# A scatter stage in which VectorE takes two steps over from GpSimd, in a new order, and a program block that ends without GpSimd's drain

## The chip, the cores and the metric

The kernel runs on one core of one Trainium2 chip. The metric is the device time in microseconds (us) of one execution. The engines are TensorE (PE in the profile; its weight loads are PEld), VectorE (DVE), ScalarE (ACT), GpSimd (POOL) and SyncE (SP, which here issues DMA transfers). Each engine runs its own instruction list in order, and the lists meet only through semaphores. A name with a q behind it (POOLq, SPq) is the engine's sequencer.

## The reference, cut to what matters

The input is x of shape (32, 128, 128): 32 batches of 128 tokens with 128 features. A graph-attention block of four rounds conditions x, then comes one transformer layer with a mixture of experts, and x is added to its result:

```python
ctx = cond(x, ...)                                   # four rounds of graph attention
a   = layernorm(ctx + mha(ctx), ln1_g, ln1_b)        # 16 heads
gp  = softmax(a @ w_group + b_group)                 # 4 groups, best one taken
ep  = softmax(einsum('td,gde->tge', a, w_expert) + b_expert)   # 2 experts in each
combine = one_hot(g_idx * 2 + e_idx) * (g_prob * e_prob)
h   = relu(einsum('td,edf->etf', a, w1) + b1)
y   = einsum('etf,efd->etd', h, w2) + b2
out = x + layernorm(a + einsum('te,etd->td', combine, y), ln2_g, ln2_b)
```

Each token uses one expert of eight. The kernel therefore sorts the tokens by expert and computes only the chosen expert for each.

## The kernel before, in words

Tokens are handled in batches of 128 (B = 32) and groups of four batches (GB = 4, G = 8). Groups are numbered 0 to 7 in the code, so G - 3 is group 5 (the sixth), G - 2 is group 6 and G - 1 is group 7. The stages are:

- The four rounds of graph attention.
- The attention of the transformer layer, a software pipeline over the batches (`for u in FLOW`). For a batch v, PE makes scores and weighs values, ACT takes exponentials (`exponentials`), DVE divides by the sums (`normalise`, L1722 and L1724), PE turns the heads (`turn_heads`, L1229, in front of it `turn_outputs`, L1224) and multiplies by the output weights with the residual (`residual`, L1238 and L1243). DVE copies that out (`residual_out`, L1733) and takes its statistics (`norm1_stats`, L1739).
- For each group of four batches: the variance (`norm1_variance`, L1744, DVE), the power -1/2 of it (`norm1_power`, L719 and L723, POOL), the normalised rows xn (`norm1_out`, L2288, ACT), and a chain of 20 small DVE steps called `route` that picks each token's expert and computes its row number `slot_i`. The links 12 and 13 (L1823, L1828) give the row number, the links 14 to 16 (L1832, L1834, L1837) the token's weight, the links 17 to 19 the running counts.
- A token's row is written to `rows`: xn times ln1_g (the x1g step), plus ln1_b (the x1 step), beside x plus bias (which `load_rows` on SP brought from DRAM) and the token's number (`group_ids`, L743). For groups 0 to 5 POOL makes x1g and x1 (L731, L734, function `rows_x1` of the gpsimd part), for groups 6 and 7 DVE (L1852, L1859, functions `rows_x1g` and `rows_x1` of the vector part). Then POOL scatters the four batches of the group into `sorted_rows` in DRAM, one indirect DMA for each (`scatter`, L761).
- The table: when five groups are counted, DVE computes where the first 13 tiles (FIRST) of 128 sorted rows lie (`tile_ends`, `tile_rows`, L1898 to L1903); POOL derives some ends from it (`taken_ends`, L832 to L845). When all are counted, DVE computes the other 26.
- The experts: 39 tiles. SP loads a tile (`load_tile`, L541), PE and ACT run the two layers, DVE adds and normalises (L2047 to L2073), and POOL scatters the tile's rows to the output with one indirect DMA (L870), 39 in all. At the very end SP waits until all of them have landed (L557), and the block ends with a barrier of all engines (its instructions carry line L117 in the profile).

All orders are written out by hand in the source. POOL's and DVE's lists behind the FLOW loop are what the change touches. SP's list at this point is: `load_rows(5)`, `load_rows(6)`, a wait for the first table, seven `load_tile`, `load_rows(7)` (it waits until group 5 is scattered), six `load_tile`, a wait for the second table and for all scatters, and the other 26.

Of the kernel before, what the change touches and what calls it, by code (L numbers as in the profile page):

```python
# [14 lines left out]
B, N, D = 32, 128, 128  # L15
TOK = B * N
GB = 4
G = B // GB
# [47 lines left out]
FIRST = -((EXPERTS * (N - 1) - COUNTED * GT) // N)  # L66
# [46 lines left out]
def build(nc, x, xT, adj, mask, weights, rowvecs, consts, ids, w1, w2, b2, out):  # L113
# [3 lines left out]
    with ExitStack() as ctx:  # L117
# [159 lines left out]
        t_base = sb("t_base", [128, FIRST])  # L277
# [117 lines left out]
        def S(name):  # L395

            if name not in sems:
                sems[name] = sem(name)
            return sems[name]
# [87 lines left out]
            copy(qkx[:, bs, :, TYPES:QK], vb[:, :, D + TYPES:D + TYPES * (1 + T_ITER)]  # L487
                 .rearrange("p b (t i) -> p b t i", i=TYPES)).then_inc(read, 1)

        block = ctx.enter_context(nc.Block())  # L490

        @block.sync
        def _(sp):
# [66 lines left out]
        def _(pool):  # L560
# [153 lines left out]
            def norm1_power(p):  # L714

                pool.wait_ge(S("mv_ready"), p + 1)
                if p >= 1:
                    pool.wait_ge(S("rstd_ready"), p)
                pool.tensor_scalar(ve[:, :], mv[:, :, 1], EPS, None, ALU.add).then_inc(S("var_ready"), 1)  # L719
                pool.wait_ge(S("var_ready"), p + 1)  # L720
                if p >= 1:
                    pool.wait_ge(S("xn_ready"), p)
                pool.tensor_tensor(rstd[:, :], ve[:, :], C("half"), ALU.pow).then_inc(S("rstd_ready"), 1)  # L723

            def rows_x1(p):

                if p == G - 3:
                    pool.wait_ge(S("on_ready"), B - 3)
                pool.wait_ge(S("xn_ready"), p + 1)
                bc = lambda n: R(n).unsqueeze(1).broadcast_to([128, GB, D])  # L730
                pool.tensor_tensor(x1_g[:, :, :], xn[:, :, :], bc("ln1g"), ALU.mult).then_inc(S("x1g_ready"), 1)  # L731
                pool.wait_ge(S("x1g_ready"), p + 1)
                pool.wait_ge(S(f"in_rows{p % 2}"), 16 * (p // 2 + 1))
                pool.tensor_tensor(rows[:, p % 2, :, 0:D], x1_g[:, :, :], bc("ln1b"), ALU.add).then_inc(S("row_x1"), 1)  # L734
# [6 lines left out]
            def group_ids(p):  # L741

                pool.tensor_copy(rows[:, p % 2, :, 2 * D + 1:2 * D + 2].bitcast(I32),  # L743
                                 id_s[:, p * GB:(p + 1) * GB].unsqueeze(2)).then_inc(S("row_ids"), 1)
# [84 lines left out]
            def taken_ends():  # L829

                pool.wait_ge(S("table_chain"), FIRST_ENDS)
                pool.memset(upto_first[:, 0:1], 0.0).then_inc(S("taken_chain"), 1)  # L832
                pool.memset(taken[:, EXPERTS:EXPERTS + 1], 0.0).then_inc(S("taken_chain"), 1)
                pool.tensor_scalar(upto_first[:, 1:EXPERTS + 1], cum[:, :], float(FIRST), None, ALU.min)\
                    .then_inc(S("taken_chain"), 1)
                pool.wait_ge(S("taken_chain"), 3)
                pool.tensor_tensor(taken[:, 0:EXPERTS], upto_first[:, 1:EXPERTS + 1], upto_first[:, 0:EXPERTS],
                                   ALU.subtract).then_inc(S("taken_chain"), 1)
                pool.wait_ge(S("taken_chain"), 4)
                pool.tensor_tensor(turn[:, :], taken[:, 1:EXPERTS + 1], taken[:, 0:EXPERTS], ALU.subtract)\  # L840
                    .then_inc(S("taken_chain"), 1)
                pool.wait_ge(S("taken_chain"), 5)
                pool.tensor_scalar(turn[:, :], turn[:, :], float(N), float(REGION), ALU.mult, ALU.add)\
                    .then_inc(S("taken_chain"), 1)
                pool.tensor_scalar(t_base_later[:, :], C("tile")[:, 0:LATER], taken[:, 0:1], float(N), ALU.add, ALU.mult)\  # L845
                    .then_inc(S("taken_chain"), 1)

            rows_x1(G - 3)
            taken_ends()
            group_ids(G - 3)  # L850
            norm1_power(G - 2)
            for n in range(GB):
                scatter(G - 3, n)
            pool.wait_ge(S("scattered0"), 16 * GB * (G // 2 - 1))
            group_ids(G - 2)
# [629 lines left out]
        def _(dve):  # L1485
# [227 lines left out]
            def normalise(v):  # L1713

                if v >= 1:
                    dve.wait_ge(S("on_ready"), v)
                if v >= 2:
                    dve.wait_ge(S("on_mm"), v - 1)
                dve.wait_ge(S("oq_mm"), v + 1)
                o = (OQ_LAST if v == B - 1 else OQ).rearrange("p (k c) -> p k c", c=STRIP)[:, :, 0:PAIR * VW].rearrange("p k (s c) -> p k s c", s=PAIR)  # L1720
                inverse = rden[:, :].rearrange("p (k s) -> p k s", s=PAIR)
                dve.reciprocal(inverse, o[:, :, :, HD]).then_inc(S("rden_ready"), 1)  # L1722
                dve.wait_ge(S("rden_ready"), v + 1)
                dve.tensor_tensor(o_n[:, v % 2, :].rearrange("p (k s c) -> p k s c", s=PAIR, c=HD), o[:, :, :, 0:HD],  # L1724
                                  inverse.unsqueeze(3).broadcast_to([128, HEADS // PAIR, PAIR, HD]), ALU.mult)\
                    .then_inc(S("on_ready"), 1)

            def residual_out(v):
                g, b = divmod(v, GB)
                if b == 0 and g >= 2:  # L1730
                    dve.wait_ge(S("xn_ready"), g - 1)
                dve.wait_ge(S("h_mm"), v + 1)
                dve.tensor_tensor(h_s[:, g % 2, b, :], head_bank(v), rowv[:, RCOLS["bo"][0]:RCOLS["bog"][1]], ALU.add)\  # L1733
                    .then_inc(S("h_ready"), 1)

            def norm1_stats(v):
                g, b = divmod(v, GB)
                dve.wait_ge(S("h_ready"), v + 1)
                dve.bn_stats(stats[:, b, :], h_s[:, g % 2, b, 0:D]).then_inc(S("stats_ready"), 1)  # L1739
# [149 lines left out]
            def tile_ends(n):  # L1889

                then(dve.tensor_reduce(cum[:, :], ntu[:, :, :], AX_X, ALU.add))
                then(dve.tensor_tensor(behind[:, 0:n, :], C("tile")[:, 0:n].unsqueeze(2).broadcast_to([128, n, EXPERTS]),
                                       row8(cum[:, :], n), ALU.is_ge))
                then(dve.tensor_reduce(t_exp[:, 0:n], behind[:, 0:n, :], AX_X, ALU.add))
# [56 lines left out]
            for u in FLOW:  # L1951
                nxt, b, more = group(u, 1)
                done, _, whole = group(u, -1)
                norm, _, normed = group(u, -2)
                if batch(u + LEAD):
                    row_tops(u + LEAD)
                if u == -1:
                    gate_centred()
                if u == 0:
                    gate_folded()  # L1960
                if batch(u - 4):
                    residual_out(u - 4)
                if b in (1, 2) and more and nxt > 0:
                    value_out(nxt, Y0, b - 1)
                if b == 2 and normed:
                    if norm == COUNTED - 1:
                        first_counts()
                    route(norm, range(12, 13))
                if u == B - GB - 1:
                    first_full(1)  # L1970
                if u == B - GB:
                    dve.wait_ge(S("st_mm"), 2 * (B - GB))
                    tile_sums()
                if batch(u - 2):
                    normalise(u - 2)
                if batch(u - 4):
                    norm1_stats(u - 4)
                if b == 0 and normed:
                    norm1_logits(norm)
                    route(norm, range(0, 6))  # L1980
                if b == 1 and normed:
                    route(norm, range(6, 12))
                if b == 2 and normed:
                    route(norm, range(13, ROUTE))
                if b == 3 and whole:
                    norm1_variance(done)
                if 1 <= u <= 4:
                    bias_parts(u - 1)
                if u == B - GB - 2:
                    first_full(0)  # L1990
                if u == B - GB - 1:
                    first_full(2)
                if u == B - GB + 1:
                    tile_ends(FIRST)
            residual_out(B - 6)
            route(G - 3, range(12, 14))
            norm1_stats(B - 6)
            normalise(B - 4)
            route(G - 3, range(14, 17))
            tile_rows(0, FIRST, t_base)  # L2000
            route(G - 3, range(17, ROUTE))

            residual_out(B - 5)
            norm1_stats(B - 5)
            norm1_variance(G - 2)
            normalise(B - 3)

            normalise(B - 2)
            norm1_logits(G - 2)
# [436 lines left out]
```

## Time and profile before

| what | value |
|---|---|
| median of 3 runs | 520.4 us (519.62 to 520.53) |
| the profiled execution's own time | 520.18 us |
| its span in the profile | 518.4 us |
| PE busy | 480.2 us (93%) |
| DVE busy | 419.3 us (81%) |
| ACT busy | 384.1 us (74%) |
| POOL busy | 274.1 us (53%) |

The span is the time from the first to the last instruction that the profile holds; 1.78 us of the execution's own time lie outside it. The busy shares are means over stages with different limits: PE is at its limit in the first 400 us, and in the last 60 us all engines are busy in turns. The page also says that the granted TensorE clock was 9 tenths or more in all slices but the last.

### The profile page before, as it was taken

To read this page: it belongs to the slowest core of one execution; us is meant where nothing else is said; L and a number is where in the kernel's file an instruction comes from. 1 tells how busy PE (TensorE), PEld (TensorE's weight loads), DVE (VectorE), ACT (ScalarE), POOL (GpSimd) and SP (SyncE) were. 2 spreads that over 40 slices of the span, in tenths; PEclk is the share of its full clock that TensorE was granted. 3 is DMA by queue.
4 is the path that set the end of the run, shared out by engine and by line. 5 is a ranking of instruction groups with operands and counts; after the bars stand their busy time and mean duration, and the time that the engine had idled before them with its cause. 6 is when DMAs were issued, how large, how long until landed. Compare 5 with 4: busy or idle time off the path is not lost. (4 is left out here: it accounts for less than half of the span.)

```text
span 518.4 us, 14957 instructions
## 1 busy us (share of the span) xinstructions
PE 480.2 (93%) x4946; PEld 327.3 (63%) x4946; DVE 419.3 (81%) x1163; ACT 384.1 (74%) x1157; POOL 274.1 (53%) x468
## 2 busy tenths in 40 slices
PE   5999999999999999999999999999999988889990
PEld 3765666766676777666545456565565655779880
DVE  2589898888888888899866768787887888899892
ACT  3779778888887888877846767677776757779990
POOL 0486673333322233302814446588887876777774
PEclk9999999999999999999999999999999999999996
DMA  8800899999999300050240000001012411555530
GB/s 344 353 2 3 258 296 301 301 292 292 295 302 295 104 0 0 2 162 1 118 126 2 3 1 3 3 33 43 24 53 54 185 44 52 151 157 146 151 106 10
DMA packets 49955, 65.64 MB, mean 127 GB/s; under 512 B 2509, under 2 KB 45522, under 8 KB 48736
## 3 DMA queue, kind: packets, MB, share of 16 engines
q1 hardware_dynamic: 47104, 58.42, 38.7%
q0 software_dynamic: 2784, 6.37, 3.5%
q8 instruction: 37, 0.61, 0.5%
q14 instruction: 30, 0.25, 0.2%
HBM read 21.04 MB, written 44.19 MB: 126 GB/s over the span
## 5 line engine op out<-in xcount | busy, mean ns | idle before, releaser
L1709 DVE TENSOR_REDUCE nm<-SC 128x8 f32<-128x1024 f32 x64 | 75.4, 1220 | 26.3 <-PE SC L1174 25.6
L2256 ACT ACTIVATE room_p<-ST 128x512 f32<-128x512 f32 (+1 forms) x96 | 64.0, 739 | 35.0 <-PE ST L1193 35.0
L1607 DVE TENSOR_REDUCE room_w<-SC 128x512 f32<-128x2048 f32 x32 | 73.0, 2281 | 1.2 <-PE SC L1001 1.2
L625 POOL TENSOR_TENSOR spread<-parts,units 128x48 bf16<-128x48 bf16 x32 | 8.8, 277 | 121.3 <-DVE parts L1582 121.3
L2162 ACT ACTIVATE room_w<-room_w,shift 128x128 f32<-128x128 f32 x128 | 49.7, 390 | 16.6 <-DVE shift L1616 16.5
L2153 ACT ACTIVATE room_w<-ST,cv 128x128 f32<-128x128 f32 x128 | 36.4, 365 | 17.7 <-PE ST L1016 17.7
L870 POOL DMA_INDIRECT out<-room_v x39 | 38.3, 982 | 12.2 <-issue 8.5
L1016 PEld LDWEIGHTS ST<-room_w 128*128 128x128 f32 x256 | 33.0, 191 | 14.2 <-issue 13.0
L761 POOL DMA_INDIRECT sorted_rows<-room_w,slot_i x32 | 33.3, 1040 | 16.2 <-issue 12.7
L2171 ACT ACTIVATE room_w<-room_w,inv 128x128 f32<-128x128 f32 x128 | 41.0, 407 | 0.1
L969 PE MATMUL ST<-room_w 128*128 128x136 f32 x256 | 40.3, 280 | 0.2 <-POOL room_w L609 0.2
L1187 PE MATMUL ST<-room_v,room_w 32*128 32x512 f32 x256 | 36.5, 638 | 2.9 <-DVE room_w L1698 1.6
L671 POOL TENSOR_TENSOR ctx_t<-room_w 128x512 f32<-128x512 f32 x24 | 30.5, 1271 | 12.0 <-PE SC L1001 8.5
L769 POOL TENSOR_TENSOR room_v<-room_w,cst 128x512 f32<-128x512 f32 x28 | 28.9, 1043 | 13.5 <-PE SC L1174 11.6
L1174 PE MATMUL SC<-room_v,room_w 32*128 32x512 f32 x256 | 35.5, 617 | 0.0
L969 PEld LDWEIGHTS ST<-room_w 128*128 128x128 f32 x256 | 34.4, 190 | 1.5 <-issue 1.5
L1016 PE MATMUL ST<-room_w 128*128 128x128 f32 x256 | 34.2, 277 | 0.9 <-issue 0.9
L1214 PE MATMUL SC<-room_p,room_w 128*32 128x128 f32 x992 | 33.5, 276 | 0.4 <-ACT room_p L2256 0.4
L1052 PE MATMUL ST<-room_w,w 128*128 128x512 f32 x64 | 33.0, 597 | 0.7 <-ACT room_w L2153 0.7
L964 PE MATMUL ST<-room_w,ctx_t 128*128 128x136 f32 x192 | 30.1, 279 | 0.0
L1214 PEld LDWEIGHTS SC<-room_p,room_w 128*32 128x32 f32 x992 | 25.2, 109 | 5.2 <-ACT room_p L2256 1.2
L1009 PEld LDWEIGHTS ST<-cst,room_w 128*128 128x128 f32 x128 | 15.5, 141 | 18.0 <-ACT room_w L2171 14.1
(340 smaller groups left out, 1327.0 us busy)
## 6 DMA issues: line engine op xcount, KB each, us to landing
sorted_rows<-w SPq DMA_DIRECT2D x8, 4290.0 KB, 38.3
room_v<-sorted_rows SPq DMA_DIRECT2D x39, 130.0 KB
x_t<-xT SPq DMA_DIRECT2D x2, 1024.0 KB, 8.2
ctx_t<-adj SPq DMA_DIRECT2D x1, 2048.0 KB, 16.8
biased_rows<-room_w SPq DMA_DIRECT2D x2, 1024.0 KB, 4.3
room_w<-biased_rows SPq DMA_DIRECT2D x8, 256.0 KB, 3.4
room_w<-mask SPq DMA_DIRECT2D x1, 1536.0 KB, 19.8
w<-weights SPq DMA_DIRECT2D x1, 1356.0 KB, 8.8
```

Of the source, the lines that this page charges most:

```text
L870: pool.indirect_dma_start(out, bass.IndirectOffsetOnAxis(ap=number, axis=0), fin[:, t % OUTS, :], None, bounds_check=TOK - 1, oob_is_err=F ...
L969: mm = pe.matmul(V[:, b, 0:D + QK], plpc[:, g % 2, b * N:(b + 1) * N], w_v[:, g % 2, b, 1, :], start=opens(s) and b in (0, 3), stop=not op ...
L1016: mm = pe.matmul(M[:, b, :], v_s[:, g % 4, b, :], prob_t[:, b, :], start=True, stop=True)
L1174: mm = pe.matmul(SC[:, r, :], q_s[at, g % 2, b * N:(b + 1) * N], k_m[at, g % 2, :, b * N:(b + 1) * N], start=True, stop=True)
L1187: pe.matmul(ST[:, r, :], k_s[at, g % 2, b * N:(b + 1) * N], q_m[at, g % 2, :, b * N:(b + 1) * N], start=True, stop=False)
L1214: mm = pe.matmul(to[STRIP * j:STRIP * (j + 1), half * N:(half + 1) * N], v_a[:, g % 2, b, at:at + STRIP], ex[:, v % 2, r, i * N:(i + 1) * ...
L1607: dve.tensor_reduce(logit[:, :, :], SC[:, :, :].rearrange("p b (i m) -> p b m i", i=TYPES), AX_X, ALU.max)\
L1709: dve.tensor_reduce(nm[:, v % 2, 2 * PER_R * pair:2 * PER_R * (pair + 1)], SC[:, 2 * pair:2 * pair + 2, :].rearrange("p r (i n) -> p (r i) ...
L2153: op = act.activation(msg_s[:, b * N:(b + 1) * N], M[:, b, :], ACT.Copy, scale=scale)
L2162: op = act.activation(expo[:, b, :], leaky[:, b, :], ACT.Exp, bias=shift[:, b:b + 1], accum_out=total[:, b:b + 1])
L2171: op = act.activation(prob[:, b, :], expo[:, b, :], ACT.Copy, scale=inv[:, b:b + 1])
L2256: act.activation(ex[:, v % 2, first:last, :], ST[:, first:last, :], ACT.Exp)\
```

## The change

The edits are:

- `Block(no_gpsimd_drain=True)`: the end of the block, a barrier of all engines, no longer has a drain on GpSimd; the other engines keep theirs.
- POOL no longer makes the x1g and x1 steps of group 5, nor waits there for `on_ready`. DVE makes them: x1g ahead of `residual_out(B - 6)`, x1 behind `norm1_stats(B - 6)` and ahead of `normalise(B - 4)`.
- On DVE `tile_rows(0, FIRST, t_base)` moves from ahead of `residual_out(B - 5)` to behind `norm1_variance(G - 2)`, and the links 17 to 19 of `route(G - 3)` move to behind `normalise(B - 3)`.
- On POOL the first scatter of group 5 moves ahead of `norm1_power(G - 2)`. `group_ids(G - 3)` gets a wait of its own until group 3 is scattered.

```diff
-        block = ctx.enter_context(nc.Block())
+        block = ctx.enter_context(nc.Block(no_gpsimd_drain=True))
...
             def rows_x1(p):
-                if p == G - 3:
-                    pool.wait_ge(S("on_ready"), B - 3)
                 pool.wait_ge(S("xn_ready"), p + 1)
...
-            rows_x1(G - 3)
             taken_ends()
+            pool.wait_ge(S("scattered1"), 16 * GB * (G // 2 - 2))
             group_ids(G - 3)
+            scatter(G - 3, 0)
             norm1_power(G - 2)
-            for n in range(GB):
+            for n in range(1, GB):
                 scatter(G - 3, n)
...
+            rows_x1g(G - 3)
             residual_out(B - 6)
             route(G - 3, range(12, 14))
             norm1_stats(B - 6)
+            rows_x1(G - 3)
             normalise(B - 4)
             route(G - 3, range(14, 17))
-            tile_rows(0, FIRST, t_base)
-            route(G - 3, range(17, ROUTE))

             residual_out(B - 5)
             norm1_stats(B - 5)
             norm1_variance(G - 2)
+            tile_rows(0, FIRST, t_base)
             normalise(B - 3)
+            route(G - 3, range(17, ROUTE))
```

## Rows read from the trace of the kernel before

**Rows 1.** Instructions at the block's end, line 117: ns min/median/max, first and last start us.

```profile
L117 POOLq DRAIN  x1: 8715/8715/8715, 509.4 to 509.4; - x1
...
L117 SPq DRAIN  x1: 13/13/13, 513.8 to 513.8; - x1
...
L117 SPq EVENT_SEMAPHORE  x1: 17/17/17, 518.3 to 518.3; - x1
```

**Rows 2.** POOL's timeline from 457 us: start us, us, instruction, idle before and releaser.

```profile
457.00 0.99 POOL L761 DMA_INDIRECT sorted_rows<-room_w,slot_i  x1 [1.12 <-DVE room_w L1837]
...
511.30 0.97 POOL L870 DMA_INDIRECT out<-room_v  x1 [0.30 <-issue]
```

**Rows 3.** DVE's timeline, its last instruction.

```profile
508.52 0.35 DVE L2068 SCALAR_TENSOR_TENSOR room_v<-room_v,rs 128x128 f32<-128x128 f32 x1
```

**Rows 4.** DVE's timeline from 435 to 443 us.

```profile
435.13 0.30 DVE L1733 TENSOR_TENSOR room_w<-SC,rowv 128x140 f32<-128x140 f32 x1 [0.79 <-PE SC L1243]
...
435.87 0.24 DVE L1722 RECIPROCAL rden<-SC 128x16 f32<-128x16 f32 x1
...
436.54 1.26 DVE L1834 SCALAR_TENSOR_TENSOR den<-ee,gs 128x4 f32<-128x4 f32 x1
...
437.93 1.33 DVE L1898 TENSOR_TENSOR room_v<-room_v,hop 128x104 f32<-128x104 f32 x1
...
439.89 0.17 DVE L1903 TENSOR_SCALAR exp_i<-t_exp 128x13 int32<-128x13 f32 x1
...
440.48 0.29 DVE L1733 TENSOR_TENSOR room_w<-SC,rowv 128x140 f32<-128x140 f32 x1
...
441.13 0.38 DVE L1744 BATCH_NORM_AGGREGATE mv<-stats 128x2 f32<-128x6 f32 x4
...
442.67 0.26 DVE L1722 RECIPROCAL rden<-SC 128x16 f32<-128x16 f32 x1 [0.69 <-PE SC L1229]
```

**Rows 5.** POOL's timeline from 434 to 444 us.

```profile
434.29 0.97 POOL L761 DMA_INDIRECT sorted_rows<-room_w,slot_i  x1 [0.30 <-issue]
436.52 1.26 POOL L731 TENSOR_TENSOR room_w<-room_w,rowv 128x512 f32<-128x512 f32 x1 [1.26 <-DVE room_w L1724]
437.86 1.28 POOL L734 TENSOR_TENSOR room_w<-room_w,rowv 128x512 f32<-128x512 f32 x1
...
440.53 0.29 POOL L845 TENSOR_SCALAR t_base_later<-cst,taken 128x26 f32<-128x26 f32 x1
...
441.92 1.05 POOL L723 TENSOR_TENSOR rstd<-ve,cst 128x4 f32<-128x4 f32 x1
443.16 1.13 POOL L761 DMA_INDIRECT sorted_rows<-room_w,slot_i  x1 [0.20 <-issue]
```

**Rows 6.** PE's timeline from 437 to 443 us.

```profile
437.50 0.40 PE L1243 MATMUL SC<-w,room_w 128*128 128x140 f32 x2
...
440.83 0.33 PE L1229 MATMUL SC<-cst,room_w 128*128 128x128 f32 x1 [1.54 <-DVE room_w L1733]
...
442.10 0.44 PE L1224 MATMUL SC<-cst,room_w 128*128 128x128 f32 x2
```

**Rows 7.** ACT's timeline, the xn rows of group 5.

```profile
429.73 1.65 ACT L2288 ACTIVATE room_w<-room_w,shift,rstd 128x128 f32<-128x128 f32 x4
```

**Rows 8.** DVE's timeline, the same operations at other places.

```profile
448.03 0.16 DVE L1834 SCALAR_TENSOR_TENSOR den<-ee,gs 128x4 f32<-128x4 f32 x1
...
452.75 0.69 DVE L1852 TENSOR_TENSOR room_w<-room_w,rowv 128x512 f32<-128x512 f32 x1
453.77 0.69 DVE L1859 TENSOR_TENSOR room_w<-room_w,rowv 128x512 f32<-128x512 f32 x1 [0.32 <-DMA room_w<-biased_rows]
...
461.23 0.34 DVE L1898 TENSOR_TENSOR room_v<-room_v,hop 128x208 f32<-128x208 f32 x1
```

**Rows 9.** POOL's timeline beside the DVE rows at 452.75 us.

```profile
452.12 0.98 POOL L761 DMA_INDIRECT sorted_rows<-room_w,slot_i  x1 [0.30 <-issue]
```

**Rows 10.** SP's timeline, the first seven tile loads.

```profile
441.06 7.71 SPq L541 DMA_DIRECT2D room_v<-sorted_rows  x7
```

## The prediction

> **What bounds the kernel now.** I read the page first, then the end of the timeline, then the waits and the timelines of each engine from 430 to 465 us, where the edits lie.
>
> The end has two parts. The first is the last step of the program. DVE's last result is ready at 508.52 + 0.35 = 508.87 [rows 3]; POOL issues the last output transfer at 511.30 and is done with it at 512.27 [rows 2]. SP, which waits until all outputs have landed, executes its own drain at 513.8. Yet the closing barrier comes at 518.3, because POOL's drain began at 509.44 and took 8.715 us, until 518.16 [rows 1]. So 4.5 us at the end are a wait of four idle engines for one drain, 4.3 of them removable if SP's 513.8 plus a short barrier becomes the end.
>
> The second part is what brings POOL to 512.27. From the scatter at 457.00 to the one at 511.30 there are 42 steps (three more scatters, 39 outputs) in 54.30 us, that is 1.293 us each against 0.97 of execution and 0.30 between two [rows 2]. POOL thus has no slack of its own from 457.00 on: the end is 457.00 plus a fixed train. The start of the train waited 1.12 us for a DVE reciprocal (the last link of group 7's route) [rows 2]. Its forerunner is DVE's list, which hardly idles from 435 on: the waits that stand there are 0.79 at 435.13, 0.69 at 442.67 and 0.32 at 453.77 [rows 4, 8]. So the bound of this stretch is DVE, and what shortens DVE between 434 and 443 should bring the whole tail forward.
>
> Two DVE instructions there are far too long. The 4-element step L1834 takes 1.26 at 436.54 and 0.16 elsewhere [rows 4, 8]. It runs in the same time as POOL's 128x512 product (436.52, 1.26) [rows 5]. The step L1898 takes 1.33 on 104 elements at 437.93, beside POOL's second product (437.86, 1.28), and 0.34 on 208 elements at 461.23 [rows 4, 5, 8]. DVE is held while POOL runs these. The excess is 1.10 and about 1.03 (I take 0.30 for 104 elements): 2.1 us.
>
> **The block's end.** The drain of POOL goes, the others stay. POOL's engine work ends at 512.27, before SP's 513.8, so SP sets the end. Between POOL's drain end (518.16) and SP's event at 518.3 lie 0.15 to 0.2 [rows 1]; the new end is 513.8 + 0.2 = 514.0. Gain 4.3. Bounds: nothing, if what the drain does is paid behind the span instead; 4.4 at most. I take 4.3, since no other instruction in the trace waits for it. The 1.78 us outside the span are taken as unchanged.
>
> **x1g on DVE.** One instruction of 0.69, about 0.71 with its hand-over [rows 8]. Its input xn is ready at 431.38 [rows 7], so it starts where DVE now idles, 434.34, and ends near 435.05. The residual copy behind it waits for PE until 435.13 anyway [rows 4]. Cost nothing; if that cover were gone, 0.7.
>
> **x1 on DVE.** 0.69 again [rows 8], between the statistics and `normalise(B - 4)`, which starts at 435.87 now [rows 4] and moves to about 436.5. It waits for the loaded rows, but link 13 ahead of it already waits for the same load. Cost 0.7. PE needs that result only behind the weighing of batch B - 2, which follows the matmuls that end at 437.90 [rows 6]; the 0.7 are hidden for PE.
>
> **POOL's products gone.** DVE loses the two holds. The route's links 14 to 16 follow: L1837 ends at 437.56, where it now ends at 438.01. DVE then reaches `residual_out(B - 5)` by 437.6. PE closes that bank at 437.50 + 0.40 = 437.90 [rows 6], so the copy starts at 438.0 and not at 440.48 [rows 4]: 2.5 us earlier, of which about 1.7 come from the table being behind it now.
>
> **PE's wait.** `turn_heads(B - 4)` sits behind that copy: PE idles 1.54 and starts at 440.83 [rows 6]. It came free at 440.83 - 1.54 = 439.29, and now finds the copy done at 438.3. The wait vanishes. Then comes `weigh(B - 1)`, about one microsecond of matmuls (it fits between the rows at 440.83 and 442.10), 439.4 to 440.5 if ACT's exponentials for it are ready, then `turn_outputs(B - 2)` at 440.6 and not at 442.10 [rows 6]. It also needs `normalise(B - 3)`.
>
> **DVE's new order.** Copy 438.0, statistics 438.3, variance 438.65 to 439.0 (0.38 [rows 4]), then the table: 0.3 + 0.3 + 0.2 + 0.1 + 0.2, done at 440.0. It ends at 439.89 + 0.17 = 440.06 today [rows 4], so the first tile loads, at 441.06 with 1.1 us each (7.71 for seven [rows 10]), neither gain nor lose. `normalise(B - 3)` follows, done at 440.5, just in time for PE at 440.6, then the links 17 to 19 until 441.0, in the time in which DVE waits for PE. `normalise(B - 2)` starts at 441.15 and not at 442.67 [rows 4]. That is the gain: 1.5 us, and what is behind it on DVE has no idle time until the first tiles.
>
> **POOL.** Its scatter of group 4 ends at 435.26 [rows 5]. `taken_ends` runs 439.14 to 440.82 now, 1.7 us [rows 5], and will run 435.3 to 437.0. The added wait for group 3's scatters is met long before (group 4's are already being issued). Then `scatter(G - 3, 0)` waits for link 16 (437.56): start about 438.4 (0.8 behind it, my value between the idle 0.20 before the scatter at 443.16 and the 1.12 before the one at 457.00 [rows 2, 5]), end 439.5. Behind this wait stand `norm1_power(G - 2)` and the other scatters. The variance is there at 439.0, the power runs 439.9 to 441.0 (1.05), where it ended at 442.97 [rows 5]. DVE wants it at about 441.65. Slack 0.6. The other three scatters end near 444.6, 3.5 us earlier than now, which also sends `load_rows(7)` out earlier and should remove most of the 0.32 for which DVE waits at 453.77 [rows 8]. That gives the end 0 to 0.3 more.
>
> **A rule that speaks against it.** DVE's product at 452.75 took 0.69 with a POOL scatter in progress from 452.12 to 453.10 [rows 8, 9]: no hold. In the Trainium skill, SBUF — State Buffer, section "SBUF: two separate sides", a VectorE copy in a two-port mode locks GpSimd out so that it cannot write descriptors (its figure, an estimate here: about 620 ns become 3,100). By that rule a scatter could be 2.5 us late; the moved steps are products of two SBUF inputs, and this trace shows no such hold, so the sum leaves it out.
>
> **The sum.** Span 518.4 - 4.3 - 1.5 = 512.6. Own time 520.18 - 5.8 = 514.4. The median lies 0.2 above the profiled execution, so 514.6.
>
> **Rivals.**
>
> - *Both as above*: 514.6. For it: each wait named is in the trace. Against it: it needs PE, POOL and DVE to be in step at 440.5 to 441. Its own range is 513.6 (reorder 2.4, the most that the variance's advance gives) to 515.6. Chance 0.62.
> - *The order gives little*: the tail hangs on something else than DVE, for example the first tile loads. Tile 0 is issued at 441.06 as before and each further one 1.1 later [rows 10], while PE would ask for them 1.5 earlier than now; no row shows when one lands, and if the loads are just in time today, this part shrinks to 0.5 or nothing. Time 515.6 to 516.2. Or the power on POOL is late by more than its slack of 0.6. Chance 0.17.
> - *The drain's time is only partly saved*, because the work it did is done outside the span. If it is paid in parallel to what else lies there, nothing of the 4.3 is gained: 520.4 - 1.5 = 518.9. For it: the drain worked 5.9 us beyond POOL's last instruction (518.16 - 512.27), and beyond SP's, so it does something real. Against it: no row says that anybody needs it. Chance 0.11. The Trainium skill, Runtime: NRT & Kernel Launch, section "The ~15µs preamble/postamble breakdown", says that a launch ends with a barrier of all engines and a re-arming of the DMA rings; no row here shows these.
> - *Slower: the same work starts only behind the barrier.* Then it is not even in parallel with the last landing. Place: right behind the span. Price 5.9 if it is the part beyond POOL's last instruction, 8.7 if the whole record. With 5.9 the time is 514.6 + 5.9 = 520.5, the same as before; with 8.7 it is 523.3. It decides from a price of 6.8 on (5.8 gained, and 1.0 to be told from no change). Chance of the same 0.06, of slower 0.04.
>
> **How the numbers follow.** A difference of 0.2% (1.0 us) is about what a measurement of this kernel tells from no change. Faster: 0.62 + 0.17 + 0.11 = 0.90, same 0.06, slower 0.04. The range: from 513.4 (reorder 2.4, and 0.2 of the load wait) to 517.5. It holds the first two cases and a drain of which a third is still paid; left out are the 0.21 of the last two rivals.
>
> **What would show it.** Right: a span of about 512.6, no POOL drain at the block's end, L1834 and L1898 at 0.16 and 0.30, the copy of batch B - 5 at 438.0, the PE wait of 1.54 gone, `normalise(B - 2)` at 441.15, the train of scatters starting at 455.4. Wrong about the end: own time minus span above 1.78 by several us. Wrong about the order: the first L1834 of the tail or DVE's `normalise(B - 2)` stays, or the train starts at 456.5 or later though DVE is early; then the tile loads or POOL's power hold it.

## The result, and the profile after

The changed kernel takes 514.28 us (median of 4 runs, 513.47 to 514.57); the kernel before took 520.07 in the same comparison. The ratio is 0.9886, with a 95% interval from 0.9869 to 0.9903: 1.1% faster. The profiled execution has a span of 512.4 and an own time of 514.35, so 1.95 lie outside the span (1.78 before).

The end of the program first. These are the instructions of line 117 in the changed kernel, as in [rows 1]:

```profile
L117 SPq EVENT_SEMAPHORE  x2: 17/17/17, 512.2 to 512.4; - x2
L117 POOLq EVENT_SEMAPHORE  x2: 17/17/17, 512.2 to 512.3; - x2
...
L117 SPq DRAIN  x1: 13/13/13, 512.1 to 512.1; - x1
```

No row of a POOL drain is left. From SP's drain at 512.1 to the end of the span are 0.3 us, where it was 513.8 to 518.4. Of the 6.0 us by which the span is shorter, 4.3 lie here and 1.7 ahead of it.

Now POOL's timeline in the changed kernel, with group 5's first scatter, the power of group 6, the first scatter of group 6, the start of the train, and the last output:

```profile
438.84 1.08 POOL L759 DMA_INDIRECT sorted_rows<-room_w,slot_i  x1 [0.89 <-POOL room_w L741]
440.00 0.25 POOL L719 TENSOR_SCALAR ve<-mv 128x4 f32<-128x4 f32 x1
440.33 1.05 POOL L723 TENSOR_TENSOR rstd<-ve,cst 128x4 f32<-128x4 f32 x1
...
449.24 1.13 POOL L759 DMA_INDIRECT sorted_rows<-room_w,slot_i  x1 [1.74 <-DVE dg L1797]
...
455.43 0.98 POOL L759 DMA_INDIRECT sorted_rows<-room_w,slot_i  x1 [0.98 <-DVE room_w L1836]
...
509.67 0.97 POOL L869 DMA_INDIRECT out<-room_v  x1 [0.31 <-issue]
```

The train starts at 455.43, 1.57 earlier than in [rows 2], and ends at 510.64, 1.63 earlier: 42 steps in 54.24 us, as before (54.30).

VectorE's timeline in the changed kernel, against [rows 4] and [rows 8]:

```profile
434.70 0.69 DVE L1851 TENSOR_TENSOR room_w<-room_w,rowv 128x512 f32<-128x512 f32 x1
435.39 0.30 DVE L1732 TENSOR_TENSOR room_w<-SC,rowv 128x140 f32<-128x140 f32 x1
...
436.13 0.68 DVE L1858 TENSOR_TENSOR room_w<-room_w,rowv 128x512 f32<-128x512 f32 x1
...
437.40 0.16 DVE L1833 SCALAR_TENSOR_TENSOR den<-ee,gs 128x4 f32<-128x4 f32 x1
...
438.20 0.30 DVE L1732 TENSOR_TENSOR room_w<-SC,rowv 128x140 f32<-128x140 f32 x1 [0.42 <-PE SC L1242]
...
439.16 0.23 DVE L1897 TENSOR_TENSOR room_v<-room_v,hop 128x104 f32<-128x104 f32 x1
...
441.32 0.26 DVE L1721 RECIPROCAL rden<-SC 128x16 f32<-128x16 f32 x1
...
452.20 0.69 DVE L1858 TENSOR_TENSOR room_w<-room_w,rowv 128x512 f32<-128x512 f32 x1 [0.47 <-DMA room_w<-biased_rows]
```

The idle 0.79 ahead of the residual copy is filled by x1g. L1833 (L1834 before) is at 0.16 where it was 1.26, and the table's first product at 0.23 where it was 1.33. The copy of batch B - 5 starts at 438.20. `normalise(B - 2)` starts at 441.32 and not at 442.67. This execution reached the stretch 0.33 us later than the one before (group 4's last scatter starts at 434.62, against 434.29 in [rows 5]), so the stretch gained 1.7. The 0.42 ahead of the copy of batch B - 5 is a new wait, for PE. The last row shows a wait that grew: 0.47 where it was 0.32.

PE in the changed kernel, against [rows 6]:

```profile
439.10 0.44 PE L1223 MATMUL SC<-cst,room_w 128*128 128x128 f32 x2
439.38 0.27 PE L1228 MATMUL SC<-cst,room_w 128*128 128x128 f32 x1
...
440.74 0.44 PE L1223 MATMUL SC<-cst,room_w 128*128 128x128 f32 x2
```

The wait of 1.54 us ahead of `turn_heads(B - 4)` is gone.

SP in the changed kernel: the load of group 6's rows and of group 5's (the first row), seven tile loads, `load_rows(7)`, the other tile loads:

```profile
421.18 16.27 SPq L524 DMA_DIRECT2D room_w<-biased_rows  x2
441.38 7.50 SPq L541 DMA_DIRECT2D room_v<-sorted_rows  x7
448.93 0.43 SPq L524 DMA_DIRECT2D room_w<-biased_rows  x1
```

The tile loads start at 441.38 (441.06 before, [rows 10]); `load_rows(7)` stands right behind the seventh.

### The profile page after: what moved, and what is told of

Same layout as the page of the kernel before. It is cut to its first block and busy times, and to the rows that moved or that the text cites. A ratio compares the mean times of both kernels' runs of the same rounds, so it can differ in the third digit from the quotient of the medians.

```text
span 512.4 us, 14960 instructions
## 1 busy us (share of the span) xinstructions
PE 480.3 (94%) x4946; PEld 327.7 (64%) x4946; DVE 418.4 (82%) x1165; ACT 383.7 (75%) x1157; POOL 271.8 (53%) x466
```

## The experiments

Times are medians; each ratio is against the kernel before on the same chip, and a gain by the ratio can differ by 0.2 us from the difference of the medians. "Rows" below means the x1g and x1 steps of group 5.

### 1. The block's end alone

The kernel before with `nc.Block(no_gpsimd_drain=True)` and nothing else.

```diff
-        block = ctx.enter_context(nc.Block())
+        block = ctx.enter_context(nc.Block(no_gpsimd_drain=True))
```

Expected:

> The kernel before with the one edit at the block's end (no GpSimd drain). Theory (the drain is a wait of its own, and nobody pays it later): span 518.4 - 4.3 = 514.1, time 4.3 us below before, some 515.8, and still 1.8 to 1.9 us between span and own time. Rival (its work moves outside the span): the span falls just as much, but own time minus span grows to 6 us and the time stays at 520. Rival (part of it was hidden by the order edits): less than 3.5 us gained here.

Measured: 515.84 against 520.22, ratio 0.9922 (0.9905 to 0.9938). The span is 513.9, the own time 515.84, so 1.94 lie outside. That is a gain of 4.4 us: all of the 4.3 are gained here, and nothing is paid later. The rival that moves the drain's work outside the span is refuted: 1.94 against 1.78 is 0.2, not 4.

### 2. The order alone, with the drain

The changed kernel with the first line of its diff taken back.

```diff
-        block = ctx.enter_context(nc.Block(no_gpsimd_drain=True))
+        block = ctx.enter_context(nc.Block())
```

Expected:

> The changed kernel with GpSimd's drain put back: all edits of order and the two steps on VectorE, nothing else. Theory (the two parts add up): 1.6 us below before, some 518.5; POOL's drain again ends about 5.9 us behind its last instruction. Rival (the order matters only because the drain is gone, as the drain started earlier hides it): no change. If the first part gave 4.3 and this 1.6, the sum is the 5.8 measured.

Measured: 519.05 (10 runs, 517.73 to 520.12), ratio 0.9977 (0.9966 to 0.9989): 1.2 us, between 0.6 and 1.8. The profile has a span of 516.5, 1.9 shorter. The two parts add up: 4.4 and 1.2 against 5.8 measured for both in the first comparison and 6.1 in the later one. The drain in this kernel:

```profile
L117 POOLq DRAIN  x1: 9318/9318/9318, 506.9 to 506.9; - x1
```

and POOL's last instruction in it:

```profile
509.40 0.97 POOL L869 DMA_INDIRECT out<-room_v  x1 [0.30 <-issue]
```

The drain ends at 516.2, 5.9 behind the end of that instruction (510.37), as before (518.16 - 512.27). Its record begins 3.5 us ahead of that end (before: 2.8), so the length of the record, 9.3 or 8.7, also holds time in which POOL still issued transfers.

### 3. Only the rows on VectorE

The kernel before, with drain, old place of the table, old order of the scatters.

```diff
-                if p == G - 3:
-                    pool.wait_ge(S("on_ready"), B - 3)
...
-            rows_x1(G - 3)
             taken_ends()
+            pool.wait_ge(S("scattered1"), 16 * GB * (G // 2 - 2))
             group_ids(G - 3)
...
+            rows_x1g(G - 3)
             residual_out(B - 6)
             route(G - 3, range(12, 14))
             norm1_stats(B - 6)
+            rows_x1(G - 3)
             normalise(B - 4)
```

Expected:

> The kernel before (drain kept, table and scatters in the old order) with only the rows of the sixth group made by VectorE, x1g ahead of residual_out(B - 6), x1 behind norm1_stats(B - 6). Theory (the holds of VectorE by POOL's products were the cost): L1834 falls to 0.16 and L1898 to 0.3 us, the table is ready at 438.8, normalise(B - 2) starts about 441.5, and 1.1 of the 1.6 us come from this edit alone. Rival (the order of table and variance is what pays): normalise(B - 2) stays near 442.5 and under 0.4 us are gained.

Measured: 518.43, ratio 0.9962 (0.9948 to 0.9975): 1.8 us by the medians, 2.0 by the ratio, more than the 1.1 expected and no less than the whole order gave. VectorE's timeline in it:

```profile
437.05 0.16 DVE L1832 SCALAR_TENSOR_TENSOR den<-ee,gs 128x4 f32<-128x4 f32 x1
...
437.34 0.23 DVE L1896 TENSOR_TENSOR room_v<-room_v,hop 128x104 f32<-128x104 f32 x1
...
438.81 0.29 DVE L1731 TENSOR_TENSOR room_w<-SC,rowv 128x140 f32<-128x140 f32 x1
...
441.00 0.26 DVE L1720 RECIPROCAL rden<-SC 128x16 f32<-128x16 f32 x1 [0.69 <-PE SC L1227]
```

The copy of batch B - 5 comes at 438.81, 0.9 later than where the changed kernel has it (438.20, less its 0.3 of lateness), and yet `normalise(B - 2)` starts at 441.00, as early. VectorE has 0.69 of idle ahead of it: PE is not ready sooner. So the new place of the table fills an idle time that costs nothing.

### 4. What holds VectorE: a first try that does not decide

The kernel before, where L1834 has one input. It leaves the factor gs out of the tokens' weights.

```diff
-                        op = dve.scalar_tensor_tensor(den[:, :], ee[:, :], 1.0, gs[:, :], ALU.add, ALU.mult)
+                        op = dve.tensor_scalar(den[:, :], ee[:, :], 1.0, None, ALU.add)
```

Expected:

> The kernel before, where L1834 (den) has one input in place of two: it leaves the factor gs out, so the tokens' weights are not the reference's. POOL's two 128x512 products stay. Theory (an instruction of VectorE with two SBUF inputs is held while POOL runs its product): L1834 takes 0.16 us, and the hold moves on to the next VectorE instruction with two SBUF inputs, L1898, or falls away where POOL's first product has ended by then; the second product then meets whatever has two inputs. Rival (VectorE is held whatever it runs): L1834 still takes 1.26.

Measured, in VectorE's timeline of this kernel:

```profile
436.68 1.26 DVE L1834 TENSOR_SCALAR den<-ee 128x4 f32<-128x4 f32 x1
437.98 0.18 DVE L1837 RECIPROCAL room_w<-den 128x4 f32<-128x4 f32 x1
438.07 1.32 DVE L1898 TENSOR_TENSOR room_v<-room_v,hop 128x104 f32<-128x104 f32 x1
```

Held as before: the theory as I put it, by the number of inputs alone, has failed. It did not decide between the number of inputs and the kind of the instruction: the one that I had put in is of another kind than the one it replaces. The reciprocal, with one input too, ran its 0.18 free, but it began at 437.98, 0.02 ahead of POOL's second product (438.00 to 439.28), so it shows little by itself.

### 5. The same with a reduction

L1834 becomes a sum over eg; the tokens' weights are again other ones.

```diff
+                        op = dve.tensor_reduce(den[:, :], eg[:, :, :], AX_X, ALU.add)
```

Expected:

> The kernel before, where L1834 (den) is a TENSOR_REDUCE over eg with its one input in SBUF, so the tokens' weights are not the reference's; the previous try used a TENSOR_SCALAR, which was held for 1.26 us too, although it has one input. Theory A (what is held is an instruction that takes VectorE's second path into SBUF: two inputs, or a TENSOR_SCALAR or copy in a faster mode; a reduction is not): L1834 takes 0.17, L1837 0.18 behind it, and L1898, now ahead of POOL's first product's end, is held until that ends (0.5 to 0.9 us). Theory B (VectorE is held whatever it runs): L1834 takes 1.26 again.

Measured. VectorE's timeline:

```profile
436.47 0.17 DVE L1834 TENSOR_REDUCE den<-eg 128x4 f32<-128x16 f32 x1
436.67 0.18 DVE L1837 RECIPROCAL room_w<-den 128x4 f32<-128x4 f32 x1
436.77 1.06 DVE L1898 TENSOR_TENSOR room_v<-room_v,hop 128x104 f32<-128x104 f32 x1
437.87 0.26 DVE L1899 TENSOR_REDUCE t_hop<-room_v 128x13 f32<-128x104 f32 x1
438.16 0.93 DVE L1900 TENSOR_TENSOR t_row<-t_hop,t_base 128x13 f32<-128x13 f32 x1
...
447.62 0.69 DVE L1852 TENSOR_TENSOR room_w<-room_w,rowv 128x512 f32<-128x512 f32 x1
...
449.97 0.16 DVE L1777 SCALAR_TENSOR_TENSOR shift<-mv,rstd 128x4 f32<-128x4 f32 x1 [0.94 <-POOL rstd L723]
```

POOL's timeline in the same kernel:

```profile
436.44 1.26 POOL L731 TENSOR_TENSOR room_w<-room_w,rowv 128x512 f32<-128x512 f32 x1 [1.26 <-DVE room_w L1724]
437.79 1.28 POOL L734 TENSOR_TENSOR room_w<-room_w,rowv 128x512 f32<-128x512 f32 x1
...
447.63 0.76 POOL L719 TENSOR_SCALAR ve<-mv 128x4 f32<-128x4 f32 x1
448.48 1.46 POOL L723 TENSOR_TENSOR rstd<-ve,cst 128x4 f32<-128x4 f32 x1
...
452.85 1.47 POOL L761 DMA_INDIRECT sorted_rows<-room_w,slot_i  x1 [0.30 <-issue]
```

Theory A holds to the number. The reduction and the reciprocal run free beside POOL's first product. The hold moves on to L1898 and ends with that product (437.83 against 437.70), and a new one falls on L1900, which ends at 439.09 with the second product (439.07). The reduction between them, L1899, runs free. So two-input instructions, and in experiment 4 the TENSOR_SCALAR, wait until POOL's product ends; reductions and reciprocals don't.

The time is 520.16, the span 518.4, as before, although VectorE was 0.67 us earlier at `normalise(B - 2)` (442.00 against 442.67). The last VectorE row says where that went: at 449.97 it waits 0.94 for POOL's power of group 7. The rows of the kernel before at this place are

```profile
449.99 0.16 DVE L1777 SCALAR_TENSOR_TENSOR shift<-mv,rstd 128x4 f32<-128x4 f32 x1 [0.22 <-POOL rstd L723]
```

for VectorE and

```profile
448.29 0.27 POOL L719 TENSOR_SCALAR ve<-mv 128x4 f32<-128x4 f32 x1
448.63 1.32 POOL L723 TENSOR_TENSOR rstd<-ve,cst 128x4 f32<-128x4 f32 x1
```

for POOL. POOL came to this power 0.66 us earlier too (447.63 against 448.29), and yet ends it at 449.94, as before (449.95). Now it is POOL that is held: VectorE's product of group 6 began at 447.62, 0.01 ahead of L719, which takes 0.76 in place of 0.27; L723, which begins during VectorE's next product, takes 1.46. In the kernel before L719 began 0.04 ahead of that product (448.33) and was free. Further on, a scatter that begins at 452.85, 0.06 behind another product of VectorE (452.79), takes 1.47 in place of 0.97. So most of what VectorE gained was lost because POOL's steps ran into VectorE's products. This experiment does not show that POOL's list by itself would have held the gain back. It shows how much slack that list has: ahead of the power of group 6 POOL waited 0.65 for VectorE's variance in the kernel before (until 441.61), and here it does not wait (440.95).

### 6. The rows alone, without the drain

The kernel of experiment 3, and

```diff
-        block = ctx.enter_context(nc.Block())
+        block = ctx.enter_context(nc.Block(no_gpsimd_drain=True))
```

Expected:

> The kernel before with the rows of the sixth group on VectorE and without GpSimd's drain, all other order as before. The run with the rows alone gave 1.8 us, the whole order 1.2. Theory (the new order of table and first scatter adds nothing to the rows): the same time as the changed kernel in this call, within 0.5 us, some 514.3. Rival (the new order adds its part): 0.5 to 1 us slower than the changed kernel.

Measured: 514.27 (513.61 to 515.48), ratio 0.9887 (0.9868 to 0.9907).

### 7. The table back in its old place

The changed kernel with

```diff
             route(G - 3, range(14, 17))
+            tile_rows(0, FIRST, t_base)
+            route(G - 3, range(17, ROUTE))
             residual_out(B - 5)
             norm1_stats(B - 5)
             norm1_variance(G - 2)
-            tile_rows(0, FIRST, t_base)
             normalise(B - 3)
-            route(G - 3, range(17, ROUTE))
```

Expected:

> The changed kernel with the first table's rows and the counts back ahead of residual_out(B - 5); the first scatter stays ahead of the power. Theory (the late table holds SP's first seven loads, and so the load of group 7's rows, for which VectorE waited 0.47 us at L1858): the first tile load goes out 1.3 us earlier, load_rows(7) at 447.2 in place of 448.9, VectorE's wait goes, and 0.3 to 0.5 us are gained on the changed kernel. Rival (the earlier variance is worth more): the variance comes 0.6 us later, the power with it, and the time is equal or 0.5 us longer.

Measured: 514.89 (514.51 to 515.32), ratio 0.9894 (0.9876 to 0.9911). VectorE's wait at L1858 is gone, as expected, but no time is gained. POOL's timeline in this kernel:

```profile
452.04 1.36 POOL L759 DMA_INDIRECT sorted_rows<-room_w,slot_i  x1 [0.30 <-issue]
453.71 0.97 POOL L759 DMA_INDIRECT sorted_rows<-room_w,slot_i  x1 [0.30 <-issue]
...
455.77 0.99 POOL L759 DMA_INDIRECT sorted_rows<-room_w,slot_i  x1 [0.88 <-POOL room_w L741]
```

and VectorE's:

```profile
451.86 0.69 DVE L1858 TENSOR_TENSOR room_w<-room_w,rowv 128x512 f32<-128x512 f32 x1
```

The earlier product now begins ahead of a scatter, and the scatter takes 1.36 in place of 0.97. It ends 0.85 behind the product's end (452.55), so it was held for 0.4. The train starts at 455.77, later than in the changed kernel. In experiment 6, with the table in its old place too, the scatter begins at 451.98, 0.05 ahead of the product (452.03), and takes 0.97.

### 8. The changed kernel again

Without any edit. Expected:

> The changed kernel itself, unchanged, for comparison on the same chip as the two above: 5.8 us below before, some 514.3, as in its first measurement.

Measured: 514.09 (513.75 to 515.80), ratio 0.9883 (0.9865 to 0.9902). So experiments 6 and 8 can't be told apart: 514.27 and 514.09, with runs 1.9 and 2.1 us apart. Experiment 7, at 514.89, lies 0.8 above this median, and five of the six runs here are faster than all of its five; the intervals of the ratios overlap, so that it is slower is likely and not shown. The theory of experiment 6 stands: the new place of the table and of the first scatter adds nothing that can be measured to the rows alone.

### 9. Group 7's rows loaded one tile earlier

```diff
-                if k == FIRST // 2:
+                if k == FIRST // 2 - 1:
                     load_rows(7)
```

Expected:

> The changed kernel, with the load of group 7's rows issued by SP behind six tile loads in place of seven. Theory (two engines are level here: VectorE's wait of 0.24 to 0.47 us at L1858 for these rows goes, but POOL's own list, four scatters, group_ids and 0.88 us until the next scatter, starts the train no earlier): VectorE's wait at L1858 gone, the train still starts within 0.2 of 455.1, time equal within 0.3 us. Rival (VectorE alone sets the train): the train starts 0.4 us earlier and the time falls by 0.4.

Measured: 514.79 (513.92 to 515.66), ratio 0.9898 (0.9880 to 0.9915). The wait at L1858 is gone, the train starts at 455.73 (expected within 0.2 of 455.1, so later than that). Again a scatter runs into the product (it takes 1.35 at 452.00, the product runs from 451.82).

### 10. And group_ids(G - 1) ahead

```diff
-            for n in range(GB):
-                scatter(G - 2, n)
+            scatter(G - 2, 0)
             pool.wait_ge(S("scattered1"), 16 * GB * (G // 2 - 1))
             group_ids(G - 1)
+            for n in range(1, GB):
+                scatter(G - 2, n)
             for n in range(GB):
                 scatter(G - 1, n)
```

Expected:

> The run above, and group_ids(G - 1) on POOL moved from behind the four scatters of group 6 to behind the first of them, so that the next scatter can follow after 0.30 us. Theory (both level engines are now relieved): the train starts at 454.5 to 454.7 in place of 455.1 to 455.4, and the time falls by 0.3 to 0.6, which the measurement can just tell. Rival (the 39 tiles of PE, ACT and VectorE are level with the train too; in the changed kernel POOL waits for VectorE's result in 22 of the 39 steps): the train starts earlier and ends as before, time unchanged.

Measured: 514.61 (513.61 to 514.89), ratio 0.9889 (0.9871 to 0.9908). The train starts at 455.39. This profiled execution was 0.47 us later than that of the changed kernel from 434 on (group 4's last scatter at 435.09 against 434.62). With that taken off, the train starts 0.5 earlier than in the changed kernel (454.9 against 455.43) and ends 0.1 earlier (511.03 less 0.47, against 510.64). That looks like the rival's picture, in which the 39 tiles on PE, ACT and VectorE are level with POOL's train and a train that starts earlier waits inside. It is not shown, though: the profile names VectorE's result as the releaser of 20 of the 39 outputs (22 in the changed kernel), but nearly all of them follow after the usual 0.30. Only two outputs waited longer, 0.60 and 0.72 (one in the changed kernel, 0.68). And the train's length differed between 53.6 and 54.7 us over the profiles of all kernels here. No version beats the changed kernel.

### 11. The drain, begun late

The changed kernel with the drain, and POOL first waits until all outputs have landed.

```diff
-        block = ctx.enter_context(nc.Block(no_gpsimd_drain=True))
+        block = ctx.enter_context(nc.Block())
...
+            for r in range(OUTS):
+                pool.wait_ge(S(f"sent{r}"), 16 * len(range(r, SLOTS, OUTS)))
```

Expected:

> The changed kernel with GpSimd's drain put back, and POOL itself waiting for all outputs to land before the drain starts (about 512.0). In four kernels the drain ended 5.9 us behind POOL's last transfer instruction. Theory (it is work of a fixed length that begins when the drain is reached and POOL is idle): the drain starts at 512.0 and takes 5 to 6 us, the span is near 518. Rival (it waits for what is still under way, and the 5.9 us count from the last transfer): it ends at 516.5 at the latest, as with the order alone, and is under 4.5 us long.

Measured: span 517.5, one run of 519.28. The drain:

```profile
L117 POOLq DRAIN  x1: 5876/5876/5876, 511.4 to 511.4; - x1
```

It starts when none of the outputs is under way any more and still takes 5.88 us. So it is not a wait for transfers. In the six kernels with the drain in its usual place it ends 5.85 to 5.9 us behind POOL's last instruction, which fits work of a fixed length that begins when POOL has finished. What this work is no run shows, nor whether its length depends on the number of transfers, which is the same in all kernels here.

### 12. POOL makes the rows, but earlier

The kernel before, with the drain and with POOL's products, without the wait ahead of them.

```diff
-                if p == G - 3:
-                    pool.wait_ge(S("on_ready"), B - 3)
```

Expected:

> The kernel before (drain kept) where POOL makes both products of group 5 itself but does not wait for on_ready first, so they run from 435.3 to 437.9 and not from 436.5 to 439.1. Theory (the hold and POOL's late list are both the cost): VectorE's instructions with two SBUF inputs between 435.3 and 437.9 are held, at most 2 us in sum as before, but POOL's list behind moves forward 1.2 us; 0.5 to 1.2 us gained. Rival (only the hold counts): the holds only move, and the time stays within 0.4 us of before.

Measured: 518.52 (11 runs, 518.21 to 519.02) against 519.94, ratio 0.9969 (0.9959 to 0.9979): 1.4 us by the medians, 1.6 by the ratio. POOL's products in it:

```profile
435.25 1.28 POOL L729 TENSOR_TENSOR room_w<-room_w,rowv 128x512 f32<-128x512 f32 x1
436.61 1.26 POOL L732 TENSOR_TENSOR room_w<-room_w,rowv 128x512 f32<-128x512 f32 x1
...
440.34 0.23 POOL L719 TENSOR_SCALAR ve<-mv 128x4 f32<-128x4 f32 x1 [0.65 <-DVE mv L1742]
```

and VectorE beside them:

```profile
435.33 0.18 DVE L1821 TENSOR_TENSOR rk<-SC,oh_h 128x32 f32<-128x32 f32 x1
...
436.53 0.16 DVE L1832 SCALAR_TENSOR_TENSOR den<-ee,gs 128x4 f32<-128x4 f32 x1
...
436.82 1.18 DVE L1896 TENSOR_TENSOR room_v<-room_v,hop 128x104 f32<-128x104 f32 x1
```

The first product meets only VectorE instructions with at most one input in SBUF (L1821 takes its other one from PSUM) and holds none. Only the second holds one, for 0.95 us. One hold of the two goes. POOL's power of group 6 starts 1.27 us earlier (440.34 against 441.61), but it still waits 0.65 for VectorE's variance, as before; so it is VectorE that came earlier, and the experiment does not separate POOL's list from the holds, as its theory had meant to. The gain is, within the intervals, what moving the rows to VectorE is worth.

## Why the prediction was right, point by point

The prediction was 514.6 us (range 513.4 to 517.5), and 514.28 was measured.

- *The block's end, 4.3.* Right: 4.4 alone, with 1.94 us between span and own time. The two rivals on the drain (0.21 together) are refuted by experiment 1. The drain takes 5.88 us even when no output is under way (experiment 11), and nothing in this program waits for what it does.
- *x1g in the idle time, x1 for 0.7.* Right: 434.70 and 436.13, the copy behind x1g not later than its bank.
- *The holds.* Right in size: 1.10 and 1.10 us are gone, where 1.10 and 1.03 were put down. That VectorE's two-input instructions are held by POOL's products is shown by experiment 5, and that the 128x512 products' place is what costs is shown by experiments 3, 6 and 12.
- *PE's wait and `normalise(B - 2)`.* Right: predicted 438.0, 440.6 and 441.15; measured 438.20, 440.74 and 441.32 in an execution that ran 0.33 late.
- *The train.* Predicted start 455.4, measured 455.43. Predicted span 512.6, measured 512.4. That the start agrees to 0.03 is chance: this execution ran 0.33 late, and two other profiles of the same order have 455.25 and 455.05 (experiments 2 and 8). The 1.5 for the reorder is confirmed only roughly: 1.2 by experiment 2, between 0.6 and 1.8, and 1.7 to 1.9 by the spans.
- *The 0.32 us of waiting for group 7's rows would mostly go.* Wrong: 0.47, and 0.24 to 0.59 in three other profiles of this order (experiments 2, 8 and 11). I let group 5's earlier scatters release `load_rows(7)`. They did end 2.9 us earlier (445.26 against 448.12), but the load is queued behind seven tile loads of 1.1 us each, and their start did not move, so it went out only 1.75 earlier (448.93 against 450.68), about as much as VectorE asked for it earlier. Had the wait gone, nothing would have been gained (experiments 7 and 9).
- *VectorE as the bound of the stretch.* Right as far as the power of group 6, where POOL waits 0.65 us for VectorE's variance both before and in experiment 12. What the reasoning lacked is the other direction: VectorE's products hold POOL's steps too, and experiment 5 lost most of its 0.67 us that way. The prediction's list of VectorE's waits also left out the 0.22 at 449.99, for POOL's power of group 7. At the start of the train the two lists are level: POOL starts it 0.88 behind its own last step in experiments 7, 8 and 9, and 0.98 and 1.14 behind it, for VectorE's reciprocal, in the changed kernel and in experiment 2.
- *The table behind the variance.* I had credited it with 1.7 of the 2.5 us by which the copy of batch B - 5 is earlier. The copy is indeed earlier, but it carries nothing on: with the table in its old place PE is ready at the same time, and the whole is equal (experiments 3 and 6). The likeliest case was right in its sum of 1.5 for the reorder, and that sum belongs to the products' removal from their place on POOL alone.
- *The rule that speaks against it.* I looked only at a VectorE product that began behind a scatter [rows 8, 9], and so took it that there is no hold. Where the product begins first, it holds the scatter: 1.47, 1.36, 1.35 and 1.24 in place of 0.97 (experiments 5, 7, 9 and 10). The Trainium skill, SBUF — State Buffer, section "Who interferes with whom", says that which of the two was issued first decides who is held; the trace agrees. The same page infers that a product of two inputs leaves descriptor generation alone; these scatters, which also read their offsets (`slot_i`) from SBUF, were held by such products for 0.3 to 0.5 us, and which part of a scatter was held no run shows. The hold is one reason why the repaired waits of experiments 7 and 9 brought nothing; the other is that POOL's own list left only 0.1 to 0.3 us to gain at the train's start (0.98 and 1.14 against 0.88).

## What to carry to other kernels

Look at the last barrier of a program as at any other wait: here GpSimd's drain cost 4.4 us there that no other engine needed. When a tiny instruction takes as long as a large one of GpSimd beside it, move the large one to a place where VectorE runs reductions or reads PSUM, or to VectorE itself; the place matters as much as the engine. A hold goes both ways: when one engine comes earlier, look at what its large instructions now run ahead of on the other. Before crediting each edit of a reorder, ask which engine is second and how much slack it has: here GpSimd's list had 0.65 us at the power of group 6 and 0.1 to 0.3 at the start of the train. GpSimd's drain was not needed in this program, and what it does is not shown; another program has to be tried without it.

## What the runs showed of the hardware that was not expected

- GpSimd's drain at the block's end takes 5.88 us with no output under way (experiment 11), and ends 5.85 to 5.9 us behind the last transfer instruction in the six other kernels with it.
- A TENSOR_SCALAR of 4 elements with one SBUF input is held by a GpSimd product as a two-input instruction is (1.26 in place of 0.17, experiment 4); a reduction and a reciprocal are not (0.17 and 0.18, experiment 5), and neither is a two-input instruction with one of its inputs in PSUM (0.18, experiment 12).
- A scatter of GpSimd that begins during a 128x512 product of VectorE ends about 0.85 us behind the product's end and takes 1.24 to 1.47 us in place of 0.97 (experiments 5, 7, 9 and 10); begun ahead of the product it takes its usual time.
- Small GpSimd instructions are held in the same way: L719 takes 0.76 us in place of 0.27 when it begins 0.01 us behind VectorE's product (experiment 5).
